# An attention and expert kernel on one core: the output bias added tile by tile in four later slots, q and k parts written projection by projection, scatters in groups of three

## The reference

```
q, k, v = split(x @ Wqkv.T + bqkv)                 # per head 16 channels
attn = softmax(q @ k.T / sqrt(16))
coh  = sigmoid(tanh(concat(x, cond) @ Wc1.T + bc1) @ Wc2.T + bc2)
mod  = attn*coh / (sum(attn*coh) + 1e-8);  mod = (1-fi)*mod + fi*fa
x1   = x + (mod @ v) @ Wout.T + bout                # bout: the output bias
gate = softmax(rms(x1)*rms_w @ wg_W + wg_b + cond @ gg_W + gg_b)
cw   = the two largest of the 8 gates, in place
out  = x1 + sum_e cw[e] * (relu(relu(x1@W1[e]+b1[e])@W2[e]+b2[e])@W3[e]+b3[e])
```

## Time and profile before

| | |
|---|---|
| median of 3 runs | 1123.45 us (1119.23 to 1123.75) |
| the profiled execution's own time | 1124.42 us |
| its span | 1122.4 us |
| mean granted TensorE clock | 0.917 |
| busy: PE, DVE, ACT, POOL | 972.4, 746.4, 549.1, 609.6 us |
| chain that ended last: PE, DVE, DMA, issue | 67%, 10%, 7%, 6% |

### The profile page before, as it was taken

The page is one execution under the profiler, slowest core; times in us unless marked ns, Lnnn a source line. Parts: engine busy times, 40 slices in busy tenths (PEclk is TensorE's granted clock), DMA queues, the critical chain, the costliest instruction groups (busy, mean ns, idle before and its releaser), DMA issues.

```text
span 1122.4 us, 24379 instructions
## 1 busy us (share of the span) xinstructions
PE 972.4 (87%) x7142; PEld 582.8 (52%) x7143; DVE 746.4 (67%) x1546; ACT 549.1 (49%) x1129; POOL 609.6 (54%) x738
## 2 busy tenths in 40 slices
PE   3789998898989889898878678989949999999993
PEld 1323333323323233232324567877838989898992
DVE  6478888786868868688874565555726656555562
ACT  2227786665857667575675344322313333333330
POOL 3324345355453445434136353767948787877874
PEclk9689999988989889899896888999969999999997
DMA  4716171513526043261254453454313232332322
GB/s 145 113 48 95 39 114 63 73 57 95 98 78 90 24 108 65 78 96 37 80 165 167 160 152 105 119 159 113 67 40 59 39 58 40 56 52 44 58 39 29
DMA packets 76527, 93.09 MB, mean 83 GB/s; under 512 B 18824, under 2 KB 69024, under 8 KB 74144
## 3 DMA queue, kind: packets, MB, share of 16 engines
q1 hardware_dynamic: 60048, 72.10, 26.9%
q0 software_dynamic: 14304, 19.15, 10.2%
q10 hardware_dynamic: 2096, 0.84, 0.3%
HBM read 60.21 MB, written 38.68 MB: 88 GB/s over the span
## 4 chain that ended last, share of the span: by engine, by line
PE 67%; DVE 10%; DMA 7%; issue 6%; ACT 5%; POOL 2%; SPq 1%; another core or an unknown queue 1%; ACTq 0%; DVEq 0%; POOLq 0%
PE bank L915 23%; PE bank L746 9%; PE bank L800 9%; PE bank L733 7%; PE bank L929 7%; ACT arena L1051 3%; PE bank L722 3%; DVE mx L1156 3%; DMA x_tile<-xs 3%; DMA out<-y,y_dest 2%; PE bank L806 2%; PE bank L874 2%; PE bank L889 2%; POOL out L615 1%; DVE arena L1420 1%
## 5 line engine op out<-in xcount | busy, mean ns | idle before, releaser
L1156 DVE TENSOR_REDUCE mx<-bank 128x1 f32<-128x512 f32 x512 | 327.2, 683 | 81.4 <-PE bank L722 56.5
L1051 ACT ACTIVATE arena<-bank 128x512 f32<-128x512 f32 x512 | 278.2, 597 | 87.7 <-PE bank L733 71.8
L608 POOL TENSOR_TENSOR hl<-hf,hh 128x256 f16<-128x256 f32 x316 | 237.8, 1121 | 128.5 <-DVE y_dest L1396 79.8
L1083 ACT ACTIVATE hf<-bank,w_b 128x256 f32<-128x256 f32 x316 | 132.5, 470 | 281.8 <-PE bank L915 277.9
L1379 DVE CAST hh<-hf 128x256 f16<-128x256 f32 x316 | 150.5, 497 | 132.4 <-ACT hf L1083 120.3
L915 PE MATMUL bank<-hh,arena 128*128 128x256 f16 x1248 | 215.7, 280 | 0.9 <-issue 0.9
L733 PE MATMUL bank<-arena 49*128 49x512 f16 x512 | 172.2, 404 | 28.6 <-issue 13.8
L722 PE MATMUL bank<-arena 48*128 48x512 f16 x512 | 173.9, 403 | 20.3 <-DVE mx L1156 20.2
L915 PE MATMUL bank<-hl,arena 128*128 128x256 f16 x624 | 174.2, 279 | 0.0
L746 PE MATMUL bank<-arena 128*17 128x512 f32 x1024 | 146.1, 644 | 0.3 <-issue 0.3
L915 PEld LDWEIGHTS bank<-hh,arena 128*128 x1248 | 125.1, 100 | 19.8 <-issue 2.5
(11 more groups left out here) (217 smaller groups left out, 1067.8 us busy)
## 6 DMA issues: line engine op xcount, KB each, us to landing
raw<-in_we SPq DMA_DIRECT2D x16, 1024.0 KB, 5.4
arena<-parts_dram SPq DMA_DIRECT2D x96, 128.0 KB, 7.1
x_tile<-xs SPq DMA_DIRECT2D x41, 256.0 KB
parts_dram<-arena SPq DMA_DIRECT2D x16, 512.0 KB
xs<-in_pads SPq DMA_DIRECT2D x8, 816.0 KB, 6.3
arena<-in_xT SPq DMA_DIRECT2D x8, 512.0 KB, 4.5
arena<-in_x SPq DMA_DIRECT2D x8, 512.0 KB, 6.0
out<-rows SPq DMA_DIRECT2D x8, 512.0 KB, 5.2
```

Source lines behind the costliest of these rows:

```text
L608: nc.gpsimd.tensor_tensor(hl[which][:, par, m, :], hf[which][:, par, m, :], hh[which][:, par, m, :], ALU.subtract).then_inc(lo[which], 1)
L1051: nc.scalar.activation(pr[:, s % TT, n, :], b_bank[no % B_RING][:, :], ACT.Exp, scale=SCALE).then_inc(b_read, 1)
L1083: nc.scalar.activation(hf[which][:, par, m, :], layer[which][m // 2][:, m % 2 * TS:(m % 2 + 1) * TS], ACT.Relu, bias=bias[which][:, bass.d ...
L1156: V.tensor_reduce(mx[:, g % 2, s % TT, c:c + 1], a_bank[no % A_RING][:, :], X, ALU.max).then_inc(a_read, 1)
```

## The change

Four things change.

1. `keep_gate_inputs` (slot 11) keeps only the copy of the gate inputs. The bias is added by `add_out_bias(i)`, one 256-column tile of the four each time, in slots 14, 15, 0 and 1 (of the next sequence). The last sequence adds all four in slot 11. A new semaphore `gates_kept` stands for the copy; `xr_ready` now counts tiles.
2. The parts are written as each projection is split: `write_parts(i, b)` in slots 10, 12, 14 and 15, two DMAs of 128 KB each time in place of two of 512 KB in slot 15. Each waits for the stack reads of the sequence before.
3. The eight scatters are split over slots 14 (three), 15 (three) and 0 (two).
4. Waits on the counts follow.

```
+BIAS_AT = {14: 14, 15: 15, 0: 16, 1: 17}
+PARTS_AT = (10, 12, 14, 15)
...
-        def write_parts(b):
-            sp.wait_ge(parts_done, 4 * b + 4)
+        def write_parts(i, b):
+            sp.wait_ge(parts_done, 4 * b + i + 1)
+            after(sp, stack_in, READS * b)
             for c in range(2):
-                sp.dma_start(parts_dram[c].rearrange("(i p) n -> p i n", p=P), parts[:, c, :, :])\
-                    .then_inc(parts_out, 16)
+                sp.dma_start(parts_dram[c][i * P:(i + 1) * P, :], parts[:, c, i, :]).then_inc(parts_out, 16)
...
-            if at == 15 and 0 <= b + 2 < B:
-                write_parts(b + 2)
+            if at in PARTS_AT and 0 <= b + 2 < B:
+                write_parts(PARTS_AT.index(at), b + 2)
...
-            nc.gpsimd.tensor_tensor(xr[:, :, 0:E], xr[:, :, 0:E], w["bo"][:, None, :].to_broadcast([P, TT, E]), ALU.add)
             pool.wait_ge(v_set, TT * (b + 1))
-            nc.gpsimd.tensor_copy(xr[:, :, E:E + NX], v[:, b % 2, :, H, 0:NX]).then_inc(xr_ready, 1)
+            nc.gpsimd.tensor_copy(xr[:, :, E:E + NX], v[:, b % 2, :, H, 0:NX]).then_inc(gates_kept, 1)
+
+        def add_out_bias(i):
+            nc.gpsimd.tensor_tensor(xr[:, i, 0:E], xr[:, i, 0:E], w["bo"][:, :], ALU.add).then_inc(xr_ready, 1)
...
+                if b == B - 1:
+                    for i in range(TT):
+                        add_out_bias(i)
...
                 targets(b - 1)
-                scatter(0, 2 * TT)
-
+                scatter(0, 3)
+            elif at == 15 and 0 <= b - 1 < B:
+                scatter(3, 6)
+            elif at == 0 and 0 <= b - 2 < B:
+                scatter(6, 2 * TT)
+            if at in BIAS_AT and 0 <= s - BIAS_AT[at] < (B - 1) * SLOTS:
+                add_out_bias(list(BIAS_AT).index(at))
+
+        scatter(6, 2 * TT)
```

More of the change, by code:

```diff
@@ L150 @@
 SPLIT_AT = {FINAL + 4 + n: (n // 4, n % 4) for n in range(4 * AHEAD)}
+PARTS_AT = (10, 12, 14, 15)
+WRITES = 16 * 2 * len(PARTS_AT)
 READS = 16 * 2 * 2 * len(Q_PARTS)
@@ L328, in model @@
     fv_set, faded, xr_ready = sem("fv_set"), sem("faded"), sem("xr_ready")
+    gates_kept = sem("gates_kept")
     squares, logit_link, logits_set, gate_exp = sem("squares"), sem("logit_link"), sem("logits_set"), sem("gate_exp")
@@ L382, in load_x @@
             sp.dma_start(xT[:, :, :], dram["xT"][:, :, b * S:(b + 1) * S]).then_inc(x_in, 16)
-        def write_parts(b):
-            sp.wait_ge(parts_done, 4 * b + 4)
+        def write_parts(i, b):
+            sp.wait_ge(parts_done, 4 * b + i + 1)
+            after(sp, stack_in, READS * b)
             for c in range(2):
-                sp.dma_start(parts_dram[c].rearrange("(i p) n -> p i n", p=P), parts[:, c, :, :])\
-                    .then_inc(parts_out, 16)
+                sp.dma_start(parts_dram[c][i * P:(i + 1) * P, :], parts[:, c, i, :]).then_inc(parts_out, 16)
         def read_stacks(b, j):
-            sp.wait_ge(parts_out, 32 * (b + 1))
+            sp.wait_ge(parts_out, WRITES * (b + 1))
             if b >= 2:
@@ L516, in split_projection @@
             evicted(pool, ("pj", i, b))
-            after(pool, parts_out, 32 * b)
+            after(pool, parts_out, WRITES * b)
             nc.gpsimd.tensor_copy(parts[:, 0, i, :], full[:, i, :]).then_inc(parts_high, 1)
@@ L1017, in take @@
                     act.wait_ge(vhalf_set, b - 1)
-                    act.wait_ge(xr_ready, b - 1)
+                    act.wait_ge(gates_kept, b - 1)
                 nc.scalar.activation(v[:, b % 2, i, :, 0:HD], m[:, 0:VW].rearrange("p (h d) -> p h d", d=HD), ACT.Copy,
@@ L1063, in split_quarter @@
             if (rank, c) == (0, 0):
-                act.wait_ge(parts_out, 32 * B)
+                act.wait_ge(parts_out, WRITES * B)
                 act.wait_ge(x_lo, B)
@@ L1116, in _ @@
             if s == FINAL + 13:
-                act.wait_ge(xr_ready, B)
+                act.wait_ge(xr_ready, TT * B)
                 take_turned(0)
@@ L1225, in take @@
             elif what == "op":
-                dve.wait_ge(xr_ready, b + 1)
+                dve.wait_ge(gates_kept, b + 1)
+                dve.wait_ge(xr_ready, TT * b + i + 1)
                 after(dve, rows_kept, 16 * b)
```

## The result

The changed kernel takes **1081.41 us** (median of 4 runs, 1079.41 to 1086.06) against 1122.84 for the kernel before (4 runs, 1119.23 to 1123.75): ratio 0.9643, 95% interval 0.9604 to 0.9682. The forecast was 1100 us, so 18.6 us of gain were not foreseen. The profiled execution took 1080.32 us, 44.1 less than that of before.

A forecast was written before the change was run, and what follows sets the result against it. It took TensorE's stops in step with GpSimd, at slot 11 and at sequence ends, as the loss: 1124.42 - 17.6 - 6.0 = 1100.8, stated as 1100 us, range 1090 to 1110, 8 in 10 within 1083 to 1113.

The forecast's parts named there:

- The hold at slot 11: Two slots around 11: moving the add frees line 1265, 12.13 to 8.40 us; 17.6 us gained over sequences 1 to 5.
- upper bound of the prediction (21.8): Two slots around 11: gain of 21.8 us if the remaining hold on line 1264 is absorbed.
- The four adds at the ends: Slots 14 to 1: four adds of 0.73 us hold nothing and `z` keeps its slack; counted 0.
- freeze: Sequence ends: TensorE stands still and its clock falls while eight scatters go out; priced at 5.4 to 7.3 us an end.
- the price of the port rule: Sequence ends: VectorE operations held by adds through the exclusive port lock; up to 13.9 us back if all 24 adds catch one.
- Scatters in groups: Six sequence ends: pauses between groups of scatters save 1.0 us each, 6.0 us together, range +7 to -26.
- the prediction's own sign: Sequence ends: the prediction called itself wrong if they change by more than 2 us either way.
- the freeze dissolves: Rival, six sequence ends: 3 to 4.4 us gained at each besides 17.6, giving 1080 to 1089 us; chance 0.2.
- The parts: Slots 10 to 15 and set-up: same bytes in 64 smaller DMAs, half leaving before the sequence's end; counted 0.

The follow-up runs named there:

- e9: The unchanged kernel before, run with its own trace on a third chip: 1090.44 us, ratio 1.0003 against the kernel before there.
- e10: The changed kernel run again, unaltered, on the third chip: 1082.71 us, ratio 0.996 against the kernel before there.
- e12: The changed kernel with the clamp of `z` ahead of the last two scatters: 1084.11 us, ratio 0.9965 against the kernel before on that chip.
- e2: The kernel before with only the parts written projection by projection; bias add in slot 11, scatters in one run: 1124.93 us, ratio 0.9998.
- e4: The changed kernel with all eight scatters in one run in slot 14, adds behind them: 1101.24 us, ratio 0.9804 against the kernel before.
- e1: The changed kernel with eight scatters in one run and parts as before, only the bias moved: 1099.17 us, ratio 0.9789 against the kernel before.
- e13: The changed kernel with its third and fourth add in slots 3 and 4 of the next sequence: 1090.37 us, ratio 0.9754 against the kernel before.
- e16: The unchanged kernel before, one run for its trace on the chip of e13: 1123.67 us.
- e11: Only the bias's adds moved, eight scatters in one run, on the third chip: 1083.0 us, ratio 0.9946 against the kernel before there.

## Why the prediction was right or wrong

**The hold at slot 11: right, sized a little low.** Line 1265 went from 2.27 to 0.19 us and the clock stayed at 1.00. The step that was off is "VectorE is nearly full there (7.19 of 7.57), so I add it: 8.40 us". The 0.83 us of hold on the first operation is still there, but the stretch lasts 7.76: VectorE is busy 7.45 of it, the hold included, and TensorE, busy 7.25, works on through it. That comes near the upper bound of the prediction (21.8): 21.0 was measured. Taking sequence 6 for the free length was sound, since it too had been run with the hold on no operation: 7.57 there, 7.76 with a projection.

**The size of the same gain on other chips: 16 instead of 21 us.** The hold is 2.27 us on both kinds, but the stretch lasts 11.00 us in e9 at clock 0.84 and 12.19 in the kernel before at 0.72. Why the clock stays low longer there was not tried.

**The four adds at the ends: wrong, "So nothing is held, and I count 0".** The reason given was VectorE and `z`. I followed only `z` behind the adds, not the field add and the transposes that wait for it, and took the slack from a stretch that the freeze had lengthened. GpSimd's 2.16 us of waiting ahead of `z` is 0.08 us in e9 (from the scatter's end at 384.60), and what stands behind, the field add, has 1.20 us there. On a frozen chip the loss is small (2.2 us in the table); without the freeze it is 7.2 us of a possible 16. "Nothing is held" was wrong by itself as well, though it cost nothing: line 1160 was placed 3 us behind the adds by a frozen trace, and in e10 an add holds it in four of the six ends, in the profile after in one. So the price of the port rule, 13.9 us, was not paid: there were four holds of 0.42 to 0.45 us, and slot 1 of e12 lasts as long without them. The rule itself, that one engine has the port pair for a whole instruction (the Trainium skill, page "SBUF — State Buffer", section "SBUF: two separate sides"), agrees with what slot 11 shows: line 1264 takes 1.02 us beside a GpSimd subtraction of 1.16, and 0.18 us in sequence 6 of the kernel before, where there is none.

**Scatters in groups: right in kind, wrong in size.** This is the term that carries most of the miss: "I take **-1.0 us** for each of six ends" was 3.4, 20.7 us together in place of 6.0. By the prediction's own sign ("if the ends change by more than 2 us either way") it was wrong here. I put three, a pause, three nearer to eight in a row than to two in a row; it was nearer to two. Of what the ends cost above those of e9 (100.9 against 68.6 us), the groups took away 20.7 of 32.3. The price was misread for one end as well: the 7.3 us of sequence 6 are not all freeze, since that end lasts 14.40 us in e9 with no freeze at all. The rival "the freeze dissolves" is nearest to what happened, two thirds of it, at 11.1 to 14.9 us for the ends of sequences 1 to 5 instead of 16.3 to 17.0; its price (3 to 4.4 us an end) and its time (1080 to 1089) were right, and its chance of 0.2 was too low. Why three in a row cost so much less, no experiment here shows. Added up against the sum of 1100.8 us for the profiled execution, which took 1080.32: 3.4 us from the slots at 11, 14.7 from the ends, 3.1 from set-up, 1.3 from the rest, less 2.2 in the other slots, is 20.3 of the 20.5.

**The parts: right at 0.** e2 stands at 0.9998 (0.9945 to 1.0051) against the kernel before, and e4, which differs from e1 by the parts alone, is 2 us slower than it, within the spread of both. Set-up gained nothing by them either.

**What none of my reasons held** is that the freeze is not the kernel's. The prediction took 5.4 to 7.3 us an end as a cost of eight scatters; on the chips of e1 to e4 and e13 to e16 it is one, and on three others it was nothing, with the kernel before and with the changed one.

## What to carry to other kernels

Slack that is read in a stretch which something else stretches is not slack: when the stretching cause goes, or the chip has none of it, the same instruction is on the path. Follow an engine's queue past the first instruction that someone needs, to the next ones; here it was the third behind the third add. And before a stall without a producer in the trace is written down as the kernel's, look at the same kernel on another chip: grouping was worth 13 us on one kind and nothing that can be measured on the other (e10 and e11, 1082.7 and 1083.0 us), while moving the bias helped on both (ratio 0.9789 in e1, 0.9946 in e11).

## What the runs showed of the hardware

The same program takes 1117.7 to 1122.8 us in one kind of chip and 1088.3 to 1089.9 us in another (medians of the kernel before). Of the 36 us between the spans of e16 and e9, 32 lie at the ends of sequences, where GpSimd issues eight indirect scatters in a row, and 5 in the two slots at 11 (the rest is 1 us shorter). At the ends it shows as starts of VectorE, ScalarE and TensorE that lag 2 to 4 us behind what they wait for, and as a granted clock of 0.79 to 0.90 instead of 1.00 in sequences 1, 2 and 4; with an operation of 0.73 us behind every third scatter the ends got 20.7 us shorter in the first comparison. In the expert stage, beside a pair of scatters, TensorE is busy for all of 5.00 us. What delays the wake-ups, and why some chips only, or only on some occasions, stays open: the same bytes pass in less time where nothing is late (DMA share 0.58 against 0.40), so traffic alone is not it, and no experiment here reaches the cause.
